# Cross-attention and FFN block on one core: score stages in one-bank halves with three banks in turn, waits at the first reader, the flag branch at another place

## The reference

```python
xn = layernorm(layernorm(x)) * gamma + beta          # the inner one without gamma, beta
q, k, v = xn @ w_q, ctx @ w_k, ctx @ w_v             # 16 heads of 64
p = softmax((q / 8) @ k.T)                           # per head, 256 x 77
x = x + tanh(gate) * (concat(p @ v) @ w_out + b_out)
g, u = layernorm(x) @ (w_gate / 127).T, layernorm(x) @ (w_up / 127).T   # 768 hidden
x = x + (silu(g) * u) @ (w_down / 127).T
```

## Time and profile before

| | |
|---|---|
| median of 3 runs | 324.16 us (323.13 to 324.96) |
| the profiled execution | 323.49 us, span 321.7 us |
| PE busy | 302.6 us, 94% of the span |
| DVE, ACT, POOL busy | 72%, 53%, 51% |
| granted PE clock, mean | 0.992 |

### The profile page before, as it was taken

One profiled execution on the slowest core, in us unless ns is written; L12 is line 12 of the kernel. 1 busy time (PEld: TensorE's weight loads), 2 busy tenths in 40 slices (PEclk: granted clock), 3 DMA queues, 4 the chain that ended last, 5 costly groups with the idle time before them and its releaser, 6 DMA issues.

```text
span 321.7 us, 6352 instructions
## 1 busy us (share of the span) xinstructions
PE 302.6 (94%) x2403; PEld 277.9 (86%) x2403; DVE 230.5 (72%) x535; ACT 171.6 (53%) x324; POOL 165.1 (51%) x163
## 2 busy tenths in 40 slices
PE   6999999988869999999999999999999899989994
PEld 6998987766868899889898989998899789978994
DVE  1498877668748778877878787878776977775543
ACT  3546873675217834862586268527734861464041
POOL 2471755168816590866196347716680767053023
PEclk9999999999979999999999999999999999999998
DMA  6992073402440013010301030121002110200000
GB/s 206 390 351 81 19 249 149 154 0 98 140 166 2 4 39 97 1 41 2 100 2 39 2 98 2 40 67 33 11 32 67 34 38 3 67 0 2 33 2 34
DMA packets 16281, 23.28 MB, mean 72 GB/s; under 512 B 1602, under 2 KB 13866, under 8 KB 16250
## 3 DMA queue, kind: packets, MB, share of 16 engines
q1 hardware_dynamic: 16250, 22.85, 21.6%
HBM read 15.87 MB, written 4.62 MB: 64 GB/s over the span
## 4 chain that ended last, share of the span: by engine, by line
PE 78%; DVE 6%; issue 4%; ACT 3%; POOL 3%; DMA 3%; SPq 0%; POOLq 0%; DVEq 0%
PE ps L708 8%; PE ps L694 7%; PE ps L756 6%; PE ps L674 5%; PE ps L757 5%; PE ps L801 5%; PE ps L802 5%; PE ps L675 5%; PE ps L803 5%; PE ps L676 5%; PE ps L599 4%; PE ps L787 3%; PE ps L786 3%; PE ps L607 2%; PE ps L577 1%
## 5 line engine op out<-in xcount | busy, mean ns | idle before, releaser
L1011 POOL TENSOR_TENSOR probs<-probs,total 128x616 f32<-128x616 f32 x32 | 38.6, 1219 | 88.3 <-DVE total L1132 88.3
L883 ACT COPY pt<-ps 77x512 f32<-77x512 f32 x64 | 34.2, 583 | 59.7 <-PE ps L694 59.7
L1027 POOL TENSOR_TENSOR h_lo<-hid,h_hi 128x256 fp32r<-128x256 f32 x48 | 35.2, 738 | 38.7 <-ACT h_hi L943 38.7
L1018 POOL TENSOR_TENSOR t_lo<-t_all,t_hi 128x1232 fp32r<-128x1232 f32 x16 | 45.6, 2849 | 4.7 <-ACT t_hi L908 4.7
L674 PE MATMUL ps<-t_hi,xn_hi 128*128 128x308 f32 x128 | 41.2, 322 | 1.2 <-ACT v_out L842 0.8
L694 PE MATMUL ps<-ident,probs 128*77 128x128 f32 x256 | 34.3, 278 | 6.6 <-issue 3.7
L675 PE MATMUL ps<-t_lo,xn_hi 128*128 128x308 f32 x128 | 39.0, 305 | 0.0
L676 PE MATMUL ps<-t_hi,xn_lo 128*128 128x308 f32 x128 | 38.9, 304 | 0.0
L694 PEld LDWEIGHTS ps<-ident,probs 128*77 128x77 f32 x256 | 30.2, 150 | 7.8 <-issue 4.9
L1116 DVE TENSOR_REDUCE top<-ps 128x8 f32<-128x616 f32 x32 | 25.5, 796 | 15.4 <-PE ps L676 14.7
L801 PE MATMUL ps<-wo_hi,o_hi 128*128 128x256 f32 x128 | 36.0, 281 | 0.3 <-issue 0.3
(11 more groups left out here) (128 smaller groups left out, 837.8 us busy)
## 6 DMA issues: line engine op xcount, KB each, us to landing
v<-v_scratch SPq DMA_DIRECT2D x8, 308.0 KB
x_ln<-in_x SPq DMA_DIRECT2D x8, 256.0 KB, 3.7
v_scratch<-v_out SPq DMA_DIRECT2D x4, 512.0 KB, 2.7
stream<-in_x SPq DMA_DIRECT2D x8, 256.0 KB, 2.7
out<-stream SPq DMA_DIRECT2D x8, 256.0 KB, 2.2
x_rooms<-in_x SPq DMA_DIRECT2D x7, 256.0 KB, 8.6
wk_raw<-in_L_xattn_w_kv SPq DMA_DIRECT2D x4, 256.0 KB, 5.7
wq_raw<-in_L_xattn_w_q SPq DMA_DIRECT2D x1, 1024.0 KB, 8.3
```

Source lines behind the costliest of these rows:

```text
L1011: nc.gpsimd.tensor_tensor(p, p, total[:, u, :].unsqueeze(2).to_broadcast([P, HG, K]), ALU.mult).then_inc(probs_done, 1)
L1018: nc.gpsimd.tensor_tensor(t_lo[:, :, cols], t_all[:, :, n, cols], t_hi[:, :, cols].bitcast(F32), ALU.subtract).then_inc(tlo_done, 1)
L1027: nc.gpsimd.tensor_tensor(h_lo[:, f, :], hid[:, f % 2, :], h_hi[:, f, :].bitcast(F32), ALU.subtract).then_inc(hlo_done, 1)
```

## The change

- Scores: each half (one bank) has its own semaphore count, and halves take banks 0, 1, 2 in turn; PE waits before each half for the subtraction three halves back. DVE reads each half with an instruction of its own.
- Shared stages take banks 6, 7 and 3 in turn, and so claim from the stage three places before.
- Waits move to the instruction that first needs the operand: hi x hi products of a stage come first; D0 waits for each slice, O0 for each pair of head groups.
- `load_ln` loads the input of b+2 in round b, behind `load_v`, where it loaded that of b+1 at the head of the round.
- The branch stands ahead of round 0, behind v9, and both bodies hold all rounds. FL moves from behind v9 to ahead of S1, BR from behind s7 to behind M0.
- The context comes first, its first three blocks apart; the first piece of the key weights is split in two, and pieces 2, 3, 4 are made behind k0, k1, k2.
- Orders of the four engines change.

```diff
-PE_ORDER = "T0 S2 T1 X1T S3 V0 XT G0 G1 T2 G2 S0 T3 G3 G4 V1 G5 S1 O0 O1 D0 D1".split()
-DVE_ORDER = "LN1 M2 LN Z2 X1 M3 O0 H0 Z3 H1 H2 M0 H3 H4 O1 H5 M1 Z0 Z1 R0 R1 AG Y0 Y1".split()
-ACT_ORDER = "Ta C0 C1 X1 E2 O0 X WO t0 E3 Tb t1 h0 t2 C2 h1 C3 t3 h2 E0 t4 O1 h3 t5 h4 h5 E1".split()
-POOL_ORDER = "P2 Ta X P3 h0 B WO h1 h2 h3 Tb h4 h5 P0 P1 XS2".split()
-SP_ORDER = "LN RES V OUT".split()
-PE_START = "v0 XT v1 v2 v3 S0 v4 S1 v5 v6 v7 v8 v9 FL".split()
-DVE_START = "LN B0 B1 B2 BC M0 s4 M1 Z0 Z1 s5 s6 s7 BR BI".split()
+PE_ORDER = "T0 S2 T1 X1T S3 V0 XT G0 G1 G2 T2 G3 S0 T3 G4 G5 V1 S1 O0 O1 D0 D1".split()
+DVE_ORDER = "LN1 M2 LN Z2 X1 M3 O0 H0 Z3 H1 H2 M0 H3 H4 O1 Z0 H5 M1 R0 Z1 R1 AG Y0 Y1".split()
+ACT_ORDER = "Ta C0 C1 E2 X1 O0 X WO t0 t1 E3 t2 h0 C2 Tb t3 h1 C3 h2 t4 E0 h3 O1 h4 t5 h5 E1".split()
+POOL_ORDER = "P2 Ta X h0 P3 B WO h1 h2 h3 h4 Tb P0 h5 P1 XS2".split()
+SP_ORDER = "RES V LN OUT".split()
+MISC_BANKS = (6, 7, 3)
+SCORE_BANKS = (0, 1, 2)
+LAST_BANKS = (0, 1, 2, 4, 5, 6)
+PE_START = "v0 XT v1 v2 v3 S0 v4 FL S1 v5 v6 v7 v8 v9".split()
+DVE_START = "LN B0 B1 B2 BC M0 BR s4 M1 Z0 Z1 s5 s6 s7 BI".split()
+CTX_FIRST = 3
+    WK_AT = (0, 1, 2, 4, 6, IC)
...
-        bank = {n: i % 2 for i, n in enumerate(shared)}
+        bank = {n: MISC_BANKS[i % len(MISC_BANKS)] for i, n in enumerate(shared)}
...
-            at = shared.index(name) - 2
+            at = shared.index(name) - len(MISC_BANKS)
...
+        def score_bank(b, u, r):
+            return SCORE_BANKS[(2 * NU * b + 2 * u + r) % len(SCORE_BANKS)]
...
-            def load_ln(n, early=False):
-                if early or n != 1:
+            def load_ln(n):
+                if n < B:
                     sp.wait_ge(xhat_done, NT * n)
                     sp.dma_start(x_ln[:], x_dram[:, n]).then_inc(xln_in, 16)
...
-            stages = {"RES": ("now", load_res), "LN": ("next", load_ln),
+            stages = {"RES": ("now", load_res), "LN": ("next", lambda n: load_ln(n + 1)),
...
+            sp.dma_start(ctx_raw[:, 0:CTX_FIRST, :], whole_rows[:, 0:CTX_FIRST, :]).then_inc(s_ctx[0], 16)
             for i in range(WP):
...
-                    pe.wait_ge(xnlo_done, b + 1)
                 if t == 0:
-                    pe.wait_ge(tlo_done, 2 * b + g + 1)
-                wait(pe, sub_done, NU * b + u - 1)
+                    pe.wait_ge(thi_done, 2 * b + g + 1)
...
                 for r in range(2):
-                    o = ps_s[:, u % 2, r, 0:BK]
+                    o = ps[:, score_bank(b, u, r), 0:BK]
+                    wait(pe, sub_done, 2 * NU * b + 2 * u + r + 1 - len(SCORE_BANKS))
                     cols = slice((g * HG + r * HB) * K, (g * HG + (r + 1) * HB) * K)
                     for c in range(DC):
                         mm(o, xn_hi[:, c, qs], t_hi[:, c, cols], start=c == 0, stop=False)
+                    if t == 0 and r == 0:
+                        pe.wait_ge(tlo_done, 2 * b + g + 1)
+                    for c in range(DC):
                         mm(o, xn_hi[:, c, qs], t_lo[:, c, cols], start=False, stop=False)
+                    if u == 0 and r == 0:
+                        pe.wait_ge(xnlo_done, b + 1)
+                    for c in range(DC):
                         ins = mm(o, xn_lo[:, c, qs], t_hi[:, c, cols], start=False, stop=c == DC - 1)
-                ins.then_inc(scores_done, 1)
+                    ins.then_inc(scores_done, 1)
...
-                    pe.wait_ge(x2lo_done, b)
...
-                    for c in range(DC):
-                        mm(o, whole(w[:, c, fs], general), whole(x2_hi[:, c, :], general), start=c == 0, stop=False)
-                        ins = mm(o, whole(w[:, c, fs], general), whole(x2_lo[:, c, :], general), start=False, stop=c == DC - 1)
+                    for x2 in (x2_hi, x2_lo):
+                        if f == 0 and at == 0 and x2 is x2_lo:
+                            pe.wait_ge(x2lo_done, b)
...
-                if t == 0:
-                    pe.wait_ge(ohi_done, NU * (b + 1))
-                    pe.wait_ge(olo_done, NU * (b + 1))
...
                 for i in range(IC):
+                    if t == 0 and i % 2 == 0:
+                        pe.wait_ge(ohi_done, NU * b + i // 2 + 1)
                     mm(o, o_hi[:, i, ts], wo_hi[:, i, :], start=i == 0, stop=False)
                     mm(o, o_hi[:, i, ts], wo_lo[:, i, :], start=False, stop=False)
+                    if t == 0 and i % 2 == 0:
+                        pe.wait_ge(olo_done, NU * b + i // 2 + 1)
...
-            first_round(PE_ORDER, stages_of(False))
             pe.wait_ge(s_flag, 2)
             inexact_here = pe.value_load(inexact[0:1, 0:1])
             with pe.If(inexact_here > 0):
+                first_round(PE_ORDER, stages_of(True))
                 other_rounds(PE_ORDER, stages_of(True))
             with pe.Else():
+                first_round(PE_ORDER, stages_of(False))
                 other_rounds(PE_ORDER, stages_of(False))
...
-                if jobs[n] == ("ctx", RC - 1):
-                    for i in range(1, WP // 2):
-                        wk_part(i)
-                if jobs[n][0] == "k" and jobs[n][1] < WP // 2:
-                    wk_part(jobs[n][1] + WP // 2)
+                if jobs[n] == ("ctx", 0):
+                    wk_part(0)
+                if jobs[n] == ("ctx", CTX_FIRST - 1):
+                    wk_part(1)
+                if jobs[n][0] == "k" and jobs[n][1] < 3:
+                    wk_part(jobs[n][1] + 2)
...
+                half = 2 * (NU * b + u)
+                psum = [ps[:, score_bank(b, u, r), 0:BK].rearrange("p (h k) -> p h k", k=K) for r in range(2)]
+                heads = [slice(r * HB, (r + 1) * HB) for r in range(2)]
+                for r in range(2):
+                    dve.wait_ge(scores_done, half + r + 1)
+                    if b > 0:
+                        dve.wait_ge(sub_done, half + r + 1 - 2 * NU)
+                    nc.vector.reduce_max(top[:, u, heads[r]], psum[r], AXIS_X).then_inc(max_done, 1)
...
+                for r in range(2):
+                    dve.wait_ge(max_done, half + r + 1)
+                    nc.vector.tensor_tensor(
+                        probs[:, u, r * BK:(r + 1) * BK].rearrange("p (h k) -> p h k", k=K), psum[r],
+                        top[:, u, heads[r]].unsqueeze(2).to_broadcast([P, HB, K]),
+                        ALU.subtract).then_inc(sub_done, 1)
```

More of the change, by code:

```diff
@@ L299, in xattn_ffn_kernel @@
         jobs += [(w, f) for w in ("wg", "wu", "wd") for f in range(FC // 2)]
-        other = 6 + 1 - bank["XT"]
+        other = MISC_BANKS[0]
         def banks_of(n):
@@ L316, in banks_of @@
                 return [other if at is None else at]
-            return [6 + bank[{m: n for n, m in stand_in.items()}[n]]]
+            return [bank[{m: n for n, m in stand_in.items()}[n]]]
         def job_of(token):
@@ L358, in gate_up_psum @@
         def gate_up_psum(b, f):
-            return ps[:, f, :] if last(b) else ps_m[:, bank[f"G{f}"], :]
+            return ps[:, LAST_BANKS[f], :] if last(b) else ps[:, bank[f"G{f}"], :]
         def rows(r):
@@ L721, in transpose_x @@
                     for t in range(NT):
-                        ins = nc.tensor.transpose(ps_m[:, bank["XT"], c * Q + t * P:c * Q + (t + 1) * P],
+                        ins = nc.tensor.transpose(ps[:, bank["XT"], c * Q + t * P:c * Q + (t + 1) * P],
                                                   x_hat[:, t, c * P:(c + 1) * P], ident[:])
@@ L732, in transpose_x1 @@
                     for t in range(NT):
-                        ins = nc.tensor.transpose(ps_m[:, bank["X1T"], c * Q + t * P:c * Q + (t + 1) * P],
+                        ins = nc.tensor.transpose(ps[:, bank["X1T"], c * Q + t * P:c * Q + (t + 1) * P],
                                                   x1_hat[:, t, c * P:(c + 1) * P], ident[:])
@@ L752, in gate_up @@
                 fs = slice(f * P, (f + 1) * P)
+                o = gate_up_psum(b, f)
                 for w, at in ((wg, 0), (wu, Q)):
-                    o = gate_up_psum(b, f)[:, at:at + Q]
-                    for c in range(DC):
-                        mm(o, whole(w[:, c, fs], general), whole(x2_hi[:, c, :], general), start=c == 0, stop=False)
-                        ins = mm(o, whole(w[:, c, fs], general), whole(x2_lo[:, c, :], general), start=False, stop=c == DC - 1)
+                    for x2 in (x2_hi, x2_lo):
+                        if f == 0 and at == 0 and x2 is x2_lo:
+                            pe.wait_ge(x2lo_done, b)
+                        for c in range(DC):
+                            ins = mm(o[:, at:at + Q], whole(w[:, c, fs], general), whole(x2[:, c, :], general),
+                                     start=x2 is x2_hi and c == 0, stop=x2 is x2_lo and c == DC - 1)
                 ins.then_inc(gu_done, 1)
@@ L919, in affine_x @@
                 for c in range(DC):
[L920 removed]
+                    nc.scalar.activation(xn[:, c, :], ps[:, bank["XT"], c * Q:(c + 1) * Q], ACT.Identity,
```

(6 more changed lines are left out.)

68 lines of the change are left out of this document (29 added, 39 removed).

## The result

The changed kernel takes **319.5 us** (319.34 to 320.88, 4 runs); the kernel before took 324.17 beside it (323.13 to 324.96, 4 runs). The ratio is 0.986, with an interval of 0.983 to 0.989. The forecast was 318.3. The profiled execution took 319.34 and spans 317.5, 4.2 less than before, where the sum had 5.8 less: the median of the runs moved by 4.7, a change of 1.4%.

A forecast was written before the change was run, and what follows sets the result against it. The prediction took PE (TensorE), busy nearly all of the span, as the bound. Its terms, -1.7 - 1.3 - 0.15 - 1.6 - 0.7 - 0.25 - 0.1 = -5.8 us, took the median from 324.16 to 318.3 us; range 315.0 to 322.6.

The forecast's parts named there:

- forecast case: Outcome in which the summed forecast holds: 316.5 to 320 us, chance 0.61.
- The branch, moved: Behind v9: load and branch run from 55.6 to 59.7, covered before T0; cost 0, bounds 0 and 0.1 us.
- The -5.96 at the old place, +4.3 behind it: Rounds 0 and 1: 4.20 waiting, 1.43 slow clock and 0.33 G1 wait go; 4.3 of new waits come; net -1.7 us.
- What is late next: Round 1: x1_hat and the input of round 2 come late; PE waits 4.0 by DVE's queue, 4.3 us taken.
- Three banks: Shared stages: G1 no longer waits for XT's bank, 0.33 in each of rounds 2 to 5, -1.3 us.
- Input ahead: Round from 242.94 falls to the usual length with its input loaded a round earlier: -1.6 us.
- Round 7: Last round: T3 waits for P3 with one G stage more done, O0 starts on V0's halves: -0.7 us.
- The start: Context first lets k0 start 1.2 earlier, but k2 waits 1.1 for key weights: -0.1 us, bounds -0.6 and +0.5.
- The tail: At the end, G0 waits for x_hi and no more for x_lo: -0.25 us, bounds -0.3 and 0.
- The first: Rival: the late input costs less in round 1, up to 3 us better, 315.3 us; chance 0.10.
- the third: Rival: P3 late behind h0 every round; mild, 0.3 a round, 320.4 us, chance 0.09; at 1.2, 326.7, chance 0.06.
- The second: Rival: branch not covered at its new place, T0 3.5 later and at the low clock, 323.2 us; chance 0.14.

The follow-up runs named there:

- experiment 3: Changed kernel with the flag load and the branch back behind round 0, all else as changed: 318.82 us.
- experiment 6: Kernel before with only the branch moved (behind v9, FL ahead of S1, BR behind M0): 323.08 us, ratio 0.996.
- experiment 5: Changed kernel with the branch back behind round 0 and the load of x(2) ahead of the write of wd: 316.49 us.
- experiment 2: Changed kernel with the old key-weight pieces, in two versions: context back at its old place, 319.03 us; context still first, 318.04 us.
- experiment 7: Kernel before with one edit, the input loaded a round ahead, behind the load of v: 322.86 us, ratio 0.995.
- experiment 8: Square around the changed kernel, three or two shared banks, new or old orders: two with new 338.34 us, three with old 320.29, two with old 321.44.
- experiment 1: Changed kernel with ACT's old order in the last pass, h0 ahead of t2: 317.8 us, ratio 0.979.

## Why the prediction came out right, point by point

- **Total.** 318.3 forecast, 319.5 measured, inside the forecast case's own range of 316.5 to 320 and on its upper side. Two terms (start and tail) failed by 2.5 us together, and the rounds from 2 on were 0.9 better than forecast. That they offset each other in part is luck.
- **The branch, moved.** The mechanism held: the sequencer ran ahead (load at 56.3, forecast 55.6), and the v products cover load and branch. The 4.0 us I gave it was 4.15 (56.3 to 60.45), since the load took 752 ns and not 490; it ends at T0's edge and costs 0.2 to 0.65, by the XT-to-T0 times, above the bound of 0.1. The Trainium skill (Advanced Engine Details and Errata, Control Flow Timing) gives a compare-and-branch some 108 ns; this branch took 3329 to 3892 ns in all fourteen traces, so for this branch the page's figure doesn't hold.
- **The -5.96 at the old place, +4.3 behind it.** The net of -1.7 came out: -4.34 and +2.53 for rounds 0 and 1, to within 0.1 of the forecast. That it did so this closely is luck: its parts were wrong. I booked all of it to the branch, and named D1's wait for the bank only as a part. But with the branch back and all other edits in place (experiment 3) these rounds are 2.1 shorter than before, and the branch alone (experiment 6) makes them 0.8 shorter and gives 0.55 back ahead of T0. So the step that failed is the -5.96 as the worth of the move: with the other edits the stall is 2.87 (experiment 5), not 5.07, and the rest would have gone anyway. That D1's bank is what did it is read from two timelines and not isolated. The slow clock of 1.43 came back once (experiment 3) and once not (5). In the changed kernel the move gained nothing: 0.7 lost by the medians with the late input (319.5 against 318.82), 0.2 won with the input early, both within noise.
- **What is late next.** Forecast: X1T 1.1, XT 1.45, G0 0.85, G3 0.4, T3 0.15. Measured: X1T 1.06 idle (1.23 by starts), XT 1.30 by starts, and G0; G3 and T3 waited for nothing. With the clock held (experiment 2) it is the forecast's queue to 0.4 each: X1T 1.23, XT 1.3, G0 0.9, G3 nothing, T3 0.4. The changed kernel has a stretch at 0.50 granted clock instead, 98.34 to 101.76, which begins behind the wait of 1.24 at XT and which no term had. The waits add to 3.94, and the clock to 0.4 to 1.0 where it falls: the 4.3, chosen between two readings, met 4.4 in this one execution.
- **Three banks.** Right in kind, too small: 0.44 a round and not 0.33, as the square shows; with it and the orders, 0.47 in a middle round of the changed kernel.
- **Input ahead.** -1.6 forecast, -1.77 measured, of which 1.27 are its own (experiment 7). It is an insurance: which round it saves is the one whose load lands late.
- **Round 7.** -0.7 forecast, -0.90 measured; 0.34 of it is the orders (experiment 8).
- **Score halves.** Cost 0, as forecast. Two halves and their subtractions:

```profile
L1140 DVE TENSOR_REDUCE top<-ps 128x4 f32<-128x308 f32 x64 | 28.8, 472 | 9.5 <-PE ps L691 9.3
```

  The forecast was 470. The Trainium skill (VectorE: DVE Perf Modes, The TRN2 errata) would give 446, an estimate from its figure for PSUM sources; the trace is 6% above. DVE is busy 23.83 in a middle round instead of 23.73.
- **The start: the term that failed first.** -0.1 forecast, +0.91 measured. The wait of k2 was as forecast (1.1; by starts 1.19), but k0 started 0.55 earlier and not 1.2, and by experiment 2 even that isn't shown to be the context's place; I took the whole lead of the context's landing for PE's. Then the branch's 0.2.
- **The tail: the term that failed most.** -0.25 forecast, +1.29 measured. I looked at what the wait for x_lo gives and noted t2 ahead of h0 as a risk for P3 only. In the last FFN ACT's queue is on the path, and the order costs about 1.5 there, with an earlier fall of the clock 1.84 (experiment 1); the rest, -0.4 to -0.55, is up to twice the gain forecast.
- **The rivals.** The first (a cheaper late input) and the third (P3 late) didn't occur, and middle rounds show no wait at T3 (round 1 has 0.24 in experiment 2). The second, an uncovered branch, occurs only at its edge.

## What to carry to other kernels

A stall that is removed from an in-order queue is worth only the distance to the next late operand, and a stall may shrink by itself when another edit lets the sequencer reach it sooner: price the edit with the others in place, and undo it alone. An order that is written for the steady round must be read again for the first and last ones, where the stages that covered it are missing. Banks and the order of claims go together: the third bank was worth 0.44 us a round with one order, and 2.3 with another, whose three claims in a row stall on two banks.

## What the runs showed of the hardware

- The load of the flag took 487 to 491 ns behind round 0 and 750 to 761 ns among the v stages; the branch took 3329 to 3892 ns, and neither place is the dearer one.
- The granted clock fell in round 1 of the changed kernel (98.34 to 101.76) and did not in a kernel that differs only in the start and has the same waits. Four traces of that round give 33.49, 33.93, 33.97 and 34.52: one execution tells the price of such a wait to 1 us.
- A load of 256 KB took 2.7 to 2.9 us or 4.1 to 4.4 us at the same place in a round, for no reason that the program gives.
